# A gated cross-attention and routed MLP layer on one Trainium2 core: keys stored with their four parts innermost, values with batch and group innermost, and new order tables

## What is computed

```python
def _L0_xattn_ref(x, y, wq, bq, wk, bk, wv, bv, wo, bo):
    q = (x @ wq + bq) ; k = (y @ wk + bk) ; v = (y @ wv + bv)      # each split into 16 heads of 16
    attn = softmax(einsum('bhqd,bhkd->bhqk', q, k) / sqrt(16))
    return einsum('bhqk,bhkd->bhqd', attn, v) merged @ wo + bo

def _L0_ffn_ref(x, gate_w, w1, b1, w2, b2, sw1, sb1, sw2, sb2):
    top1 = argmax(softmax(x @ gate_w.T))                           # one of 2 experts for each token
    masked = x where the expert is the chosen one, 0 elsewhere
    routing = sum over e of relu(masked[e] @ w1[e] + b1[e]) @ w2[e] + b2[e]
    return routing + relu(x @ sw1 + sb1) @ sw2 + sb2               # hidden width 1024

x = x + tanh(g_xattn) * _L0_xattn_ref(layernorm(x), ctx, ...)
x = x + tanh(g_ffn) * _L0_ffn_ref(layernorm(x), ...)
```

## Time and profile before

| | us |
|---|---|
| three runs, median (lowest to highest) | 339.07 (337.38 to 339.97) |
| the profiled execution, its own time | 337.8 |
| its span in the profile | 336.0 |

### The profile page before, as it was taken

One profiled execution on the slowest core, in us unless ns is written; L12 is line 12 of the kernel. 1 busy time (PEld: TensorE's weight loads), 2 busy tenths in 40 slices (PEclk: granted clock), 3 DMA queues, 4 the chain that ended last, 5 costly groups with the idle time before them and its releaser, 6 DMA issues.

```text
span 336.0 us, 7284 instructions
## 1 busy us (share of the span) xinstructions
PE 315.3 (94%) x2383; PEld 282.6 (84%) x2383; DVE 225.8 (67%) x516; ACT 214.4 (64%) x483; POOL 185.7 (55%) x264
## 2 busy tenths in 40 slices
PE   7889978999999999999999999959999999999993
PEld 6567756679988797987998889949999999999992
DVE  5699997999689888894819639753433544444463
ACT  2635998989696675759795358515547547555742
POOL 6355789673673948636550776612355536535542
PEclk9999998999999999999999999987999999999998
DMA  5872831361010040001000681305056243203300
GB/s 140 270 236 53 264 30 19 73 135 25 7 19 2 16 160 0 2 1 67 0 2 5 198 266 66 126 32 189 2 217 209 56 172 94 70 26 94 94 31 28
DMA packets 31780, 29.37 MB, mean 87 GB/s; under 512 B 16398, under 2 KB 28690, under 8 KB 31243
## 3 DMA queue, kind: packets, MB, share of 16 engines
q1 hardware_dynamic: 27974, 21.05, 22.2%
q0 software_dynamic: 2656, 7.32, 6.5%
q10 hardware_dynamic: 1125, 0.67, 0.7%
HBM read 16.15 MB, written 7.96 MB: 72 GB/s over the span
## 4 chain that ended last, share of the span: by engine, by line
PE 72%; DVE 6%; POOL 5%; issue 3%; ACT 3%; ACTq 0%; DVEq 0%; POOLq 0%
PE y_ps L1540 25%; PE h_ps L1540 19%; PE s_ps L1540 10%; PE bank L1540 9%; PE bank L1679 4%; PE bank L1715 1%; PE bank L1782 1%; POOL probs L686 1%; POOL nt L727 1%; DVE smax L1252 1%; DVE probs L1264 1%; DVE rsum L1270 1%; DVE h L1511 1%; ACT probs L950 1%; DVE hT_lo L1518 1%
## 5 line engine op out<-in xcount | busy, mean ns | idle before, releaser
L1540 PE MATMUL y_ps<-sw,hT_hi 128*128 128x256 f32 x272 | 57.0, 292 | 0.9 <-DVE hT_lo L1518 0.6
L1474 DVE TENSOR_TENSOR hT_lo<-h,hT_hi 128x256 fp32r<-128x256 f32 x64 | 29.9, 467 | 37.2 <-ACT h L1091 37.2
L1540 PE MATMUL y_ps<-ew,hT_hi 128*128 128x256 f32 x256 | 52.9, 285 | 0.0
L686 POOL TENSOR_TENSOR probs<-probs,rinv 128x616 f32<-128x616 f32 x32 | 39.4, 1246 | 22.6 <-DVE rinv L1273 22.4
L1540 PEld LDWEIGHTS y_ps<-sw,hT_hi 128*128 128x128 f32 x272 | 44.7, 191 | 2.8 <-DVE hT_lo L1518 1.9
L1540 PE MATMUL h_ps<-x2T_hi,sw 128*128 128x512 f32 (+1 forms) x160 | 43.8, 361 | 0.0
L1540 PEld LDWEIGHTS y_ps<-ew,hT_hi 128*128 128x128 f32 x256 | 42.3, 189 | 0.1
L1540 PE MATMUL y_ps<-sw,hT_lo 128*128 128x256 f32 x136 | 38.4, 282 | 0.0
L1540 PE MATMUL y_ps<-ew,hT_lo 128*128 128x256 f32 x128 | 36.0, 281 | 0.0
L1000 ACT ACTIVATE hT_hi<-h_ps,vec_cols 128x512 fp32r<-128x512 f32 (+1 forms) x40 | 24.4, 610 | 17.6 <-PE h_ps L1540 13.1
L960 ACT ACTIVATE pT<-bank 128x512 f32<-128x512 f32 x40 | 23.8, 606 | 18.4 <-PE bank L1679 18.1
(11 more groups left out here) (208 smaller groups left out, 825.1 us busy)
## 6 DMA issues: line engine op xcount, KB each, us to landing
stage<-in_L_ffn_w SPq DMA_DIRECT2D x4, 1024.0 KB, 5.9
sw<-ew SPq DMA_DIRECT2D x4, 1024.0 KB, 5.2
xs<-sorted_dram SPq DMA_DIRECT2D x8, 257.0 KB, 3.1
stage<-in_L_ffn_sw SPq DMA_DIRECT2D x2, 1024.0 KB, 7.1
x_all<-in_x SPq DMA_DIRECT2D x1, 1536.0 KB, 7.0
...
```

The source lines that it names most:

```text
L686: nc.gpsimd.tensor_tensor(pq, pq, inverse, ALU.mult).then_inc(p_ready, 1)
L1474: nc.vector.tensor_tensor(hT[1][:, c % HB, 0:RTOK], h32[:, c % 2, 0:RTOK], hT[0][:, c % HB, 0:RTOK], ALU.subtract).then_inc(h_lo, 1)
L1540: return nc.tensor.matmul(out_, lhsT, rhs, start=start, stop=stop, **kw)
```

## The change

The four parts of a key lie beside each other: `k_parts`, `k_dram` and `k_own` have the part as the last axis. One of a head's transfers thus moves 16 runs of 1,232 bytes where it moved 64 runs of 308 bytes. TensorE reads one part of `k_own` as every fourth number, 16 bytes apart. ScalarE and GpSimd write the parts in the same steps, and `k32` keeps its order.

Batch and group (4 by 2) are the last axis of `v32`, `v_pair` and `v_left`. The runs of the values' transfers are 512 bytes (16 numbers by 8) where they were 64 bytes. The stationary operands of `attend` are read with a step of 8 numbers, 32 bytes. The copy of the values out of PSUM is two instructions of ScalarE for each two batches where it was one, and writes with the step of 8. The products that make the values write PSUM in runs of 16 numbers.

All five order tables are new. Nothing that is computed changes.

```diff
-    warm.0 yt.0 yt.1 yt.2 yt.3 vt warm.1 kp.0.0 kp.0.1 kp.1.0 kp.1.1 vp.0 in.0.0 vp.1 vp.2 in.1.0 qy.0.1 vp.3 sc.0.0
...
-    kw.0 kw.1 kr.1 kr.2 wd.0 wd.1 vr.0 kr.3 kr.4 fl.0 wd.3 vr.1 kr.5 kr.6 kr.7 wd.2 wd.4 wd.5 ps.0 ps.1 ps.2 xs ps.3
+    kw.0 kw.1 kr.1 kr.2 vr.0 wd.0 wd.1 kr.3 kr.4 wd.3 vr.1 wd.2 kr.5 kr.6 ps.0 kr.7 wd.4 wd.5 ps.1 ps.2 xs fl.0 ps.3
...
-    k_dram = nc.dram_tensor("k_dram", (P, 2 * GROUPS, BATCHES * KEYS), F32).ap()
+    k_dram = nc.dram_tensor("k_dram", (P, BATCHES, KEYS * 2 * GROUPS), F32).ap()
...
-        k_own = sb("k_own", [P, 2, 2 * GROUPS, HH, KEYS], F32R, scope=att)
+        k_own = sb("k_own", [P, 2, HH, KEYS, 2 * GROUPS], F32R, scope=att)
...
-        v_pair = sb("v_pair", [P, 2, BATCHES, GROUPS * HP, PD], scope=att)
-        v_left = sb("v_left", [P, BATCHES, GROUPS, P], scope=att)
+        v_pair = sb("v_pair", [P, 2, 2, HP, PD, VALUE_BATCHES * GROUPS], scope=att)
+        v_left = sb("v_left", [P, 2, P, VALUE_BATCHES * GROUPS], scope=att)
...
         k32 = xn2[:, :, :, :].rearrange("p a t r -> p (a t r)")[:, 0:GROUPS * GK].rearrange(
-            "p (g n) -> p g n", g=GROUPS)
-        k_parts = probs[:, 1, :, :].rearrange("p q n -> p (q n)").rearrange("p (m g n) -> p m g n", m=2, g=GROUPS)
+            "p (g b k) -> p g b k", g=GROUPS, k=KEYS)
+        k_parts = probs[:, 1, :, :].rearrange("p q n -> p (q n)").rearrange(
+            "p (b k c) -> p b k c", b=BATCHES, k=KEYS)
...
-                cols = slice(half * YH, (half + 1) * YH)
-                sp.dma_start(k_dram[:, :, cols], k_parts[:, :, :, cols].rearrange("p m g n -> p (m g) n")
-                             ).then_inc(k_out[half], 16)
+                batches = slice(half * BATCHES // 2, (half + 1) * BATCHES // 2)
+                sp.dma_start(k_dram[:, batches, :].rearrange("p b n -> p (b n)"),
+                             k_parts[:, batches, :, :].rearrange("p b k c -> p (b k c)")).then_inc(k_out[half], 16)
 
...
-                    sp.dma_start(k_own[rows, n, :, h % HH, :].bitcast(F32), k_dram[rows, :, b * KEYS:(b + 1) * KEYS]
+                    sp.dma_start(k_own[rows, n, h % HH, :, :].rearrange("p k c -> p (k c)").bitcast(F32), k_dram[rows, b, :]
                                  ).then_inc(k_in[n], 16)
...
-                    heads = v32[share][key:key + rows, half, :, :].rearrange("k b (c q f) -> k (b c) q f", q=2, f=HEAD_DIM)
-                    cols = slice(parity * HEAD_DIM, (parity + 1) * HEAD_DIM)
-                    sp.dma_start(v_pair[to:to + rows, half, batches, :, cols].rearrange("p b c f -> p (b c) f"),
-                                 heads[:, :, parity, :]).then_inc(v_in[share], 16)
+                    head = slice(parity * HEAD_DIM, (parity + 1) * HEAD_DIM)
+                    sp.dma_start(v_pair[to:to + rows, half, share, :, head, :].rearrange("p i f n -> p i (f n)"),
+                                 v32[share][key:key + rows, parity, half * HP:(half + 1) * HP, :, :].rearrange(
+                                     "k i f n -> k i (f n)")).then_inc(v_in[share], 16)
...
-                    left = v32[share][key:key + LEFT, half, :, :].rearrange("k b (g d) -> k (b g) d", g=GROUPS)
                     for i in range(HP):
-                        first = (2 * i + 1 - half) * HEAD_DIM
+                        first = half * HR + (2 * i + 1 - half) * HEAD_DIM
                         rows = slice(half * HP * LEFT + i, (half + 1) * HP * LEFT, HP)
-                        sp.dma_start(v_left[rows, batches, :, half * HR + first:half * HR + first + HEAD_DIM].rearrange(
-                                     "p b g f -> p (b g) f"), left[:, :, first:first + HEAD_DIM]).then_inc(v_in[share], 16)
+                        sp.dma_start(v_left[rows, share, first:first + HEAD_DIM, :].rearrange("p f n -> p (f n)"),
+                                     v32[share][key:key + LEFT, 1 - half, half * HP + i, :, :].rearrange("k f n -> k (f n)")
+                                     ).then_inc(v_in[share], 16)
...
-                cols = slice(half * YH, (half + 1) * YH)
-                nc.gpsimd.tensor_tensor(k_parts[:, 1, g, cols].bitcast(F32R), k32[:, g, cols], k_parts[:, 0, g, cols],
-                                        ALU.subtract).then_inc(k_lo, 1)
+                batches = slice(half * BATCHES // 2, (half + 1) * BATCHES // 2)
+                nc.gpsimd.tensor_tensor(k_parts[:, batches, :, GROUPS + g].bitcast(F32R), k32[:, g, batches, :],
+                                        k_parts[:, batches, :, g], ALU.subtract).then_inc(k_lo, 1)
...
-                cols = slice(half * YH, (half + 1) * YH)
-                to = k_parts[:, 0, g, cols].bitcast(F32R) if rounded else k32[:, g, cols]
-                nc.scalar.activation(to, key_bank(half, g), ACT.Copy).then_inc(k_hi if rounded else k_32, 1)
+                batches = slice(half * BATCHES // 2, (half + 1) * BATCHES // 2)
+                to = k_parts[:, batches, :, g].bitcast(F32R) if rounded else k32[:, g, batches, :]
+                nc.scalar.activation(to, key_bank(half, g).rearrange("p (b k) -> p b k", k=KEYS), ACT.Copy).then_inc(k_hi if rounded else k_32, 1)
...
-                nc.scalar.activation(v32[2 * j // VALUE_BATCHES][:, :, at:at + 2, :].rearrange("k m n d -> k n m d"),
-                                     value_bank(j).rearrange("k (n m d) -> k n m d", n=2, m=2), ACT.Copy
-                                     ).then_inc(v_32, 1)
+                own = slice(at * GROUPS, (at + 2) * GROUPS)
+                for q in range(2):
+                    ins = nc.scalar.activation(
+                        v32[2 * j // VALUE_BATCHES][:, q, :, :, own].rearrange("k x f n -> k x n f"),
+                        value_bank(j).rearrange("k (x n q f) -> k x n q f", x=2 * HP, n=2 * GROUPS, q=2)[:, :, :, q, :], ACT.Copy)
+                ins.then_inc(v_32, 1)
...
-                        ins = mm(value_bank(j)[:, n * DIM:(n + 1) * DIM], yT[rows, k, b * KEYS:(b + 1) * KEYS],
-                                 wv_sb[rows, k, :].rearrange("p (g m d) -> p m g d", g=GROUPS, m=2), k == 0,
+                        ins = mm(value_bank(j).rearrange("k (x n d) -> k x n d", x=2 * HP, n=2)[:, :, n, :], yT[rows, k, b * KEYS:(b + 1) * KEYS],
+                                 wv_sb[rows, k, :].rearrange("p (g x d) -> p x g d", g=GROUPS, x=2 * HP), k == 0,
...
-                                     k_own[rows, b % 2, km * GROUPS + g, :, :].rearrange("p h k -> p (h k)"), n == 0, n == 2)
+                                     k_own[rows, b % 2, :, :, km * GROUPS + g].rearrange("p h k -> p (h k)"), n == 0, n == 2)
...
-                        mm(bank[m][cols, g * SEQ:(g + 1) * SEQ], v_pair[:, i // HP, b, g * HP + i % HP, :],
+                        mm(bank[m][cols, g * SEQ:(g + 1) * SEQ], v_pair[:, i // HP, b // VALUE_BATCHES, i % HP, :, b % VALUE_BATCHES * GROUPS + g],
...
-                    ins = mm(bank[m][:, g * SEQ:(g + 1) * SEQ], v_left[0:ROWS[PAIRS], b, g, :],
+                    ins = mm(bank[m][:, g * SEQ:(g + 1) * SEQ], v_left[0:ROWS[PAIRS], b // VALUE_BATCHES, :, b % VALUE_BATCHES * GROUPS + g],
```

102 lines of the change are left out of this document (51 added, 51 removed).

## The result

| | before | changed |
|---|---|---|
| median of 13 runs (lowest to highest) | 339.77 us (337.38 to 343.44) | 342.77 us (340.20 to 347.36) |
| the profiled execution, its own time | 337.8 us | 340.91 us |
| its span | 336.0 us | 339.2 us |

The ratio is 1.0079, with a 95% interval of 1.0045 to 1.0113: the changed kernel is 0.8% slower. It is taken over the fast runs of both kernels, those within 1.5% of the fastest, so it isn't quite the quotient of the two medians. The forecast was 342.8 us.

What follows compares the result with a forecast made beforehand. TensorE, busy 94% of the span and full from 77 to 190 us, was taken as the bound. Terms +7.4 + 1.5 - 3 - 0.7 - 1.5 = +3.7 us gave a median of 342.8 us, range 332.5 to 350 us.

Steps and rivals of the forecast that it cites:

- three signs of being wrong: Moving step free, moving step costing more than 0.23 us a pair, or the time of h.0.0 moving by over 3 us.
- The keys' reading in the full stage: TensorE's stepped k_own reads in 16 quarters of batches 4 to 7: 0.46 us each, +7.4 us (0 to +22).
- The choice between the ends: Price of TensorE's stepped key read: 0.5 ns a column taken, between 0 and 1.5 ns.
- free step: Rival for TensorE's key reads: the moving operand's step costs nothing, only the order counts, 333.9 us; 32%.
- cost by length: Rival for TensorE's key reads in 28 quarters: price grows with distance, 462 ns a pair, 367 us; 8%.
- The early quarters: Stepped key reads in 12 quarters of batches 1 to 3: 5.5 us added against 5.4 us idle, +1.5 us (0 to +11).
- The order around `va.0`: Batch 0's product with its values, before 77 us: va.0 fills TensorE's gap, -3 us (-1 to -4).
- The cover of that move: Shorter value transfers, out before 41 us, let va.0 move earlier; issued as slowly as before, they land about 50 us.
- Of the shorter transfers I take the gain as 0.: Key and value transfers: shorter issue gains 0 by itself, since no wait showed at their first readers.
- The opening: Before the first scores: qy.0 fills the 1.59 us wait of in.1 for ScalarE, -0.7 us (0 to -1.5).
- The seam: 220 to 230 us, ahead of the routed work: shorter waits and some clock regained, -1.5 us (0 to -3.5).
- stall rival: Seam's reads hold TensorE for sorted rows not landed: 2 to 3 us stall at 217 us, 346 us; new wait 10%.

Runs made afterwards that it cites:

- e1: The changed kernel with the score products reading 308 neighbouring numbers of k_own instead of every fourth (wrong numbers); 0.9804 of the kernel before.
- e3: The changed kernel with the score products reading every third number of k_own (wrong numbers); one run, 343.21 us.
- e8: The changed kernel with va.0 put back behind sc.2.2 on TensorE; 1.0185 of the kernel before.
- e6: The kernel before with the five new order tables, keys and values in the old layout; 0.9907 of the kernel before.
- e11: The kernel before with the new order tables and ScalarE's fourth value copy (vpe.3) moved up behind the third; 0.9892 of the kernel before.
- e12: The kernel before with only va.0 moved ahead of sc.2.2 and the first share of values ahead of the MLP's weights; 1.0052 of the kernel before.
- e5: The changed kernel with the five old order tables, so the new layout alone; 1.0302 of the kernel before.
- e7: The changed kernel with the keys alone in their old layout, values and orders as changed; 0.9835 of the kernel before.
- e4: The changed kernel with the table reads and first sorted rows' transposes (xst) put back behind y.4.7 on TensorE; 1.0073 of the kernel before.
- e9: The changed kernel itself, measured a second time; 1.0084 of the kernel before.

## Why the prediction was right, and where its steps were off

The forecast, +3.7 us on the profiled execution, stands against +3.2 us of span, and 342.8 us against 342.77 us. The second agreement is luck in part: the median of the kernel before also moved, from 339.07 us to 339.77 us with more runs, and several terms were off by 1 to 2.5 us in ways that cancelled. The mechanism, that the stepped reading in the full stage outweighs what the orders save, was the forecast one, shown by e1 to e3. None of the three signs of being wrong came: a pair costs 0.13 us more, and `h.0.0` moved by 0.8 us, a little less than the 1 to 3 us said. The terms:

- **The keys' reading in the full stage, +7.4 us.** 0.39 us for a quarter where 0.46 us were taken, so 6.2 us. The choice between the ends, that any step costs the same and is worth about one more pass, was right; "0.5 ns for a column" was 0.42 ns (0.13 us for a pair's 308 columns). The row it came from, a stationary load, was a fair guide in size, but that was luck in part: the reason given, that the distance doesn't matter, is shown for the moving operand alone. The stationary loads of `v_left` pay 146 ns for 128 columns at a step of 8, against the row's 64 ns at a step of 2. The rivals of the free step (32%) and of the cost by length (8%) are refuted.
- **The early quarters, +1.5 us.** In the new orders 2.1 us (e1 against changed). In the old orders it is 4.0 us. That TensorE had as much idle time as the quarters added did not mean that they fell into it.
- **The order around `va.0`, -3 us.** Mis-sized: without the two moved steps 2.6 us in the old layout and 4.8 us in the new one. The step that failed is "no reordering can take more than its 4.0 idle us out of it": VectorE's idle time in the old layout was no bound for the new one, where the slower TensorE adds waits of its own, and where taking back one step costs 5.9 us (e8). Also "the granted clock" was named and not priced; in e8 it halves TensorE's rate for 10 us. Together with the term above, from `sc.1.0` to `h.0.0`: 4.0 - 4.8 = -0.8 us, and -1.8 us with the moved work, forecast -1.5 us. The two errors, of 2.5 and 1.8 us, cancelled.
- **The cover of that move.** I argued that the shorter transfers made it possible, and that at the old pace the values would land at 50 us. e6, e11 and e12 show that they would not. The old pace needed both the short runs and the place behind the weights: ahead of the weights the short runs take 9.29 us (e6), and in e5 the long runs keep their pace right behind them:

```profile
33.32 3.60 SPq L496 DMA_DIRECT2D v_pair<-v_first  x4
36.97 3.21 SPq L504 DMA_DIRECT2D v_left<-v_first  x4
```

That is 6.86 us. The layout was not needed for the order.
- **"Of the shorter transfers I take the gain as 0."** Right for the changed kernel. I had not seen the second share's tie to the tile `h`, which makes TensorE wait 2.2 + 0.9 us once the score products are fast (e6), and 0.4 + 0.9 us with the longer runs (e7).
- **The opening, -0.7 us.** Not seen: `in.1` waits 1.33 and 0.57 us in the two profiles of the changed kernel, in place of 1.59 us, but another 0.39 us has come, and the first products of the values wait 1.37 and 1.59 us for ScalarE in place of 0.45 us. `sc.1.0` starts 0.7 to 1.0 us later, of which 0.6 us are the transposes `in.2` that now stand ahead of it; they wait 0.56 us for ScalarE. Its spread over profiles is larger than the term.
- **The seam, -1.5 us.** The two gaps shrank by 1.4 us, forecast 0.8 us, and the clock is full. What was wrong is "the two reads take 1.7 us and stay on TensorE": the gap ahead of the transposes is 0.79 us, and 0.21 us in e4, where the table was made long before the reads. The gap ahead of the routed work is 1.71 us, forecast 1.4 us. By start times the first 24 routed products take 2.2 us less, but all of the routed work only 1.2 us less, with 0.67 us of a new wait in it (0.6 us less in e9). With 2.1 to 2.6 us together the term was too small in the profiles. Its stall rival, reads that hold TensorE for rows that haven't landed, did not come.
- **The issue of the transfers** got shorter, from 0.72 to 0.53 us for each key transfer, and the values were out at 38.9 us, before the 41 us forecast.
- **Two slips in the rivals' numbers**, without effect. The terms' bounds give 330.1 to 338.1 us for the free step, and not 331.4 to 339.1 us; and a stall of 2 to 3 us at 48 us in place of -3 gives some 348 us, where 346 us fits the seam's case alone.
